# Reordering GpSimd's work in the turns of an attention stage: scatters without holds, the variance's power first

## The reference, cut to what matters

```
# stage 7, x is (8, 512, 256), 16 heads of 16
q = heads(layernorm(x) @ Wq.T + bq); k, v = heads(ctx @ Wk.T + bk), heads(ctx @ Wv.T + bv)
x = x + tanh(g_xattn[3]) * (softmax(q @ k.T / 4) @ v @ Wo.T + bo)
# stage 8
y = rmsnorm(layernorm(x)) * rms_w
vals, idx = top_k(y @ gate_w.T, 2); w = softmax(vals)
out = layernorm(x) + sum over the two experts e of w[e] * ((silu(y @ W1[e]) * (y @ W2[e])) @ W3[e])
x = x + tanh(g_ffn[3]) * out
```

## Time and profile before

| | |
|---|---|
| median of 3 runs | 2703.14 us (2701.21 to 2703.17) |
| the profiled execution, its own time | 2703.14 us |
| its span, first to last instruction | 2701.3 us |
| TensorE busy | 2433.2 us (90%) |
| VectorE busy | 1356.8 us (50%) |
| ScalarE busy | 943.6 us (35%) |
| GpSimd busy | 575.0 us (21%) |
| mean granted TensorE clock | 0.949 |
| stage 7 in the span | about 1837 to 2090 us |

### The profile page before, as it was taken

The page is one execution under the profiler, slowest core; times in us unless marked ns, Lnnn a source line. Parts: engine busy times, 40 slices in busy tenths (PEclk is TensorE's granted clock), DMA queues, the critical chain, the costliest instruction groups (busy, mean ns, idle before and its releaser), DMA issues.

```text
span 2701.3 us, 39252 instructions
## 1 busy us (share of the span) xinstructions
PE 2433.2 (90%) x13940; PEld 1598.6 (59%) x13940; DVE 1356.8 (50%) x3016; ACT 943.6 (35%) x2203; POOL 575.0 (21%) x544
## 2 busy tenths in 40 slices
PE   7997999999989987986999889986995899999998
PEld 4444766666666654444666654543553577777776
DVE  7886654754554556874222643336885323232322
ACT  2466555443444432321222212224553222222221
POOL 3234222440000102102321000002345212111111
PEclk9999999999999998997999669998996899999999
DMA  5013001220001102000000039302014322221221
GB/s 186 1 40 98 17 9 48 69 80 24 24 24 32 39 12 77 1 1 16 0 0 8 25 125 332 102 0 102 33 64 182 106 32 33 36 33 32 32 35 26
DMA packets 73747, 144.42 MB, mean 53 GB/s; under 512 B 11592, under 2 KB 62536, under 8 KB 71120
## 3 DMA queue, kind: packets, MB, share of 16 engines
q1 hardware_dynamic: 41280, 100.94, 10.9%
q0 software_dynamic: 16368, 26.23, 4.9%
q10 hardware_dynamic: 15936, 15.03, 2.0%
HBM read 107.42 MB, written 71.09 MB: 66 GB/s over the span
## 4 chain that ended last, share of the span: by engine, by line
PE 75%; DVE 10%; issue 6%; ACT 5%; DMA 1%; POOL 1%; another core or an unknown queue 0%; ACTq 0%; DVEq 0%; SPq 0%; POOLq 0%
PE PS L1959 12%; PE PS L1981 7%; PE PS L1382 4%; PE PS L1392 4%; PE PS L2347 4%; PE PS L1706 3%; PE PS L1717 3%; PE PS L564 3%; PE PS L2359 3%; PE PS L2381 3%; PE PS L2407 2%; PE PS L2442 2%; PE PS L2416 2%; PE PS L2452 2%; PE PS L639 2%
## 5 line engine op out<-in xcount | busy, mean ns | idle before, releaser
L1959 PE MATMUL PS<-mem,ctx2T 128*128 x1136 | 350.0, 461 | 2.1 <-ACT ctx2T L2022 1.1
L1959 PEld LDWEIGHTS PS<-mem,ctx2T 128*128 128x128 f32 x1136 | 211.4, 191 | 108.9 <-issue 4.3
L2141 POOL DMA_INDIRECT out_x<-xnT,moe_small x71 | 110.2, 1552 | 483.7 <-ACT xnT L2036 483.7
L1981 PE MATMUL PS<-mem,moe_small 128*128 x852 | 195.7, 379 | 1.1 <-DVE moe_small L2113 1.1
L2105 DVE TENSOR_TENSOR ctx2T<-PS,ctx2T 128x352 f32<-128x352 f32 x142 | 74.5, 524 | 243.1 <-PE PS L1959 243.1
L1981 PEld LDWEIGHTS PS<-mem,moe_small 128*128 128x128 f32 x852 | 156.4, 190 | 19.9 <-issue 1.4
L1056 DVE RECIPROCAL mem<-PS 128x512 f32<-128x512 f32 x48 | 160.8, 3350 | 12.6 <-PE PS L633 12.2
L2737 DVE TENSOR_REDUCE moe_small<-PS 128x2 f32<-128x1024 f32 x64 | 78.5, 1226 | 143.5 <-PE PS L2407 143.5
L2574 ACT ACTIVATE mem<-PS,moe_small 128x512 f32<-128x512 f32 x128 | 86.7, 682 | 158.2 <-DVE moe_small L2737 131.2
L1051 DVE TENSOR_REDUCE mem<-PS 128x32 f32<-128x2048 f32 x48 | 109.9, 2289 | 61.9 <-PE PS L589 61.7
L2110 DVE COPY moe_small<-PS 128x512 f32<-128x512 f32 x71 | 49.1, 691 | 173.2 <-PE PS L1969 173.2
(11 more groups left out here) (362 smaller groups left out, 4699.6 us busy)
## 6 DMA issues: line engine op xcount, KB each, us to landing
slots<-in_trash_rows SPq DMA_DIRECT2D x8, 4290.0 KB, 62.7
mem<-in_L_ffn_experts SPq DMA_DIRECT2D x8, 2176.0 KB, 8.9
xn<-unit_rows SPq DMA_DIRECT2D x15, 512.0 KB, 3.9
xn<-slots ACTq DMA_DIRECT2D x53, 130.0 KB, 2.1
x_all<-in_x SPq DMA_DIRECT2D x8, 512.0 KB, 8.3
mem<-unit_rows SPq DMA_DIRECT2D x8, 512.0 KB
out_x<-x_all ACTq DMA_DIRECT2D x8, 512.0 KB
unit_rows<-moe_small SPq DMA_DIRECT2D x7, 512.0 KB, 3.2
```

Of the source, the lines that this page charges most:

```text
L1959: last = nc.tensor.matmul(PS[:, 1 + 2 * g + half, 0:HE], m.rowT[:, j % 2, k, :], w[:, :, at:at + HE], start=k == 0, stop=k == KD - 1)
L1981: last = nc.tensor.matmul(PS[:, 7, 0:D], m.hT[:, j % 2, n, :], w[:, :, at:at + D], start=n == 0, stop=n == KE - 1)
L2141: nc.gpsimd.indirect_dma_start(s.T["out"], bass.IndirectOffsetOnAxis(s.token[:, j % 4:j % 4 + 1], 0), m.result[:, j % 4, :], None, compute ...
```

## The change

In the loop over the turns at the end of `xattn_pool`, `norm_powers` moves to the front of the turn and `scatter` up behind `row_ends`, ahead of `xn_scales` and `add_bias`. The two waits in the middle go: the one that let the first three scatters start only when TensorE had finished both of the turn's scores, and the one that let the other five start only when it had finished the shifted scores of the batch before. The eight scatters are one call.

```diff
     for n in range(s.turns):
         now, before, old, route, place = turn_of(s, n)
+        if route:
+            norm_powers(n - 3)
         if place:
             row_ends(n - 4)
+            scatter(n - 4, 0, 2 * TB)
         for b in STATS_IN_TURN.get(n, ()):
             xn_scales(b)
         if n + 1 < B:
             add_bias(n + 1)
-        if route:
-            norm_powers(n - 3)
-        if place:
-            if now:
-                pool.wait_ge(s.sems["scores"], 2 * n + 2)
-            scatter(n - 4, 0, 3)
-            if before:
-                pool.wait_ge(s.sems["shifted_psum"], 2 * n)
-            scatter(n - 4, 3, 2 * TB)
```

## The result

The changed kernel takes 2718.22 us (median of 4 runs, 2716.63 to 2719.6), the kernel before 2702.62 us (4 runs, 2701.21 to 2703.17): 1.0062 times, 95% interval 1.005 to 1.0075, some 16 us slower. The prediction was 2701.2 us with a range up to 2708.0: wrong. The profiled execution of the changed kernel took 2725.52 us, 7 us more than the median, so its sizes are too large: a later profile of the same kernel under the same conditions (2719.07 us) shows the stretches of turns 4 to 6 shorter by 0.7 to 3.2 us.

What follows compares the result with a forecast made beforehand. TensorE holds 75% of the last chain; results stall until the last scatter is dealt with. Turns 4 to 6: -4.5 + 4.5 = 0, turn 7 -1.4, turn 8 -0.5: -1.9 from 2703.14, 2701.2 us; range 2694.9 to 2708.

Steps and rivals of the forecast that it cites:

- Parts 1 and 2: GpSimd's turn: `norm_powers` first starts when it did, and nobody waits for `row_ends` behind it; worth 0 each.
- Part 3: Unheld scatters end 2.5 us earlier, so the stall goes: 1.5 us in each of turns 4 to 6, 1.4, then 0.5.
- Part 4: Turns 4 to 6: `add_bias` behind the scatters holds L1128 for 2.2 us, paying back 1.5 us a turn.
- Part 5: Turn 10: some 1.9 us of VectorE's wait for the power go without reaching the end; worth 0, at most 0.5.
- (c): Eight scatters in a row hold TensorE's results where all wait: +7.5, 2710.6 us; chance 0.16, with a clock loss.
- (b): Turns 4 to 8: the stall doesn't hang on the scatters' end and stays, hiding L1128's block: 2703.1 us; chance 0.14.
- (d): TensorE's clock after turn 5: shifted idle moves a half-speed stretch 1 to 2 us either way; loss shares (c)'s 0.16.
- (a): `add_bias` comes just after L1128, the stall still goes: -6.4, 2696.7 us; chance 0.22 all free, 0.12 partly.

Runs made afterwards that it cites:

- quiet comparisons: Three of six comparisons, those where the unaltered kernel before takes 2695 us; the changed kernel there takes 1.0035 and 1.0021 times that kernel's time.
- late comparisons: Three of six comparisons, the first measurement among them, where the unaltered kernel before takes 2702 to 2703 us; the changed kernel there takes 1.0062 times.
- The copies: Changed kernel plus SyncE copying 2.1 MB between DRAM tensors beside the scatters in turns 4 to 7: 2718.54 us, 1.0063 times the kernel before.
- bias_inside: Changed kernel with `add_bias` put between the second and third scatter, no holds: 1.0 times the kernel before (0.999 to 1.0009), 0.0 us.

## Why the prediction was wrong, step by step

**Parts 1 and 2 (power first, `row_ends` behind it: 0).** Right. The power starts when the variance is there, after an idle 18.18 us. The first scatter starts 11.95 us after the turn's first `add_out`, where the working had 1939.9 - 1928.37 = 11.5.

**Part 3 (holds removed: the stall goes, -6.4 us over turns 4 to 8).** This is the step that failed. Its arithmetic held: the scatters end 21.96 us after that `add_out` (predicted 21.5), and the pairs of L1066 are 1.64 us apart. But it took the 1.5 us that the kernel before showed for the whole effect, and asked only whether the results of the old place would be free in time. The effect is that TensorE's signals can arrive late while scatters run, in other places too. Once unheld, the scatters start ahead of the second scores' end, and the signals of these, of the sums and of the transposes come 2.7 to 5.3 us later than in the kernel before, one behind the other in the chain, and in part of the stretches the clock falls on top. The stretches of turns 4 to 6 became 8.3, 6.9 and 7.0 us longer in the profiled execution and 5.6, 3.7 and 6.3 in the later one, where 1.5 us were to go. In one comparison the removed holds alone cost 30.6 us (27 and 34 in its two runs), the order with the holds 0.5 us. In the quiet comparisons the step fails in another way: there is no stall to gain on. Two of the signs that the prediction named for being wrong came in the first profile: ScalarE waited longer, and L1128 took 0.19 us.

**Part 4 (`add_bias` behind the scatters blocks L1128 for 2.2 us).** The mechanism was right, and the first measurement didn't show it: there L1128 came at 1956.45 us instead of 1950.24, `add_bias` ran beside L1056 and L1059, and L1128 took 0.19 us. In the quiet comparisons it is the whole loss: L1124 loses 2.81 us, in turn 5 L1113 2.27 us. So the victim was named two instructions too late. The price, +1.5 us a turn, looked at `add_out` alone, where VectorE's wait of 0.77 us between the pairs takes up part of the block. That wait does go, but TensorE's rank matmuls (L673) wait for L1128 too: in four turns for 5.8 us, where the kernel before has one such wait of 2.5, and the stretch of turn 5 is granted a clock of 0.93. The turns pay 2.75, 2.33 and 1.91 us. With -1.9 us as the sum of the whole, the forecast would have missed the quiet +5.3 and +7.6 us as well.

The rule of the Trainium skill that the prediction cites here names a second input in SBUF as what makes the conflict; L1124, L1113 and L1149 agree. L1100 has one input, and lost 1.88 us. For this the same section of the Trainium skill ("SBUF — State Buffer", Who interferes with whom) says that `tensor_scalar` can enter a mode that uses both ports, and the row agrees.

**Part 5 (turn 10: 0).** Right. The power comes first, at 2094.92 us, and the first load of rows at 2122.47 us is 29.6 us behind the expert loads (before: 29.4). The timeline of turn 10:

```profile
2092.86 1.85 SPq L1906 DMA_DIRECT2D mem<-in_L_ffn_experts  x4
...
2094.92 1.68 POOL L1235 TENSOR_TENSOR moe_small<-moe_small 128x8 f32<-128x8 f32 x1 [8.00 <-DVE moe_small L1142]
```

**The rivals.** (c) came true in its kind and its sign; it had 0.16 together with a loss by the clock. Its place was wrong: it looked at the end of the row of scatters, "among the transposes of the maxima" (L601), and the late signals are those of L589, L633 and L652, 6 to 9 us ahead of it. It also kept the old stall, which went. Its price of 1.5 us a turn was the visible remainder of a late signal, where the holds had kept the rest away. The evidence against it, turn 10's eight scatters from 2076.32 us without a pause, is sound as far as it goes. The timeline of TensorE there, in the kernel before:

```profile
2081.62 3.58 PE L662 MATMUL PS<-moe_small,x_all 128*128 128x8 f32 x16 [0.78 <-ACT x_all L859]
```

The logits are over at 2085.20, and ScalarE reads them at 2085.24, with the scatters running; in the changed kernel turn 10 has no late signal either. So scatters alone don't make a signal late. Turn 10 differs in that TensorE stands still most of the time, and whether that is what matters wasn't tried. (b) fell in the late comparisons, since the stall went when the scatters moved. The rule of the Trainium skill quoted with it, that TensorE and ScalarE never wait for another's access, is neither borne out nor refuted: TensorE's matmuls kept their distances, and what came late is their results or the news of them. (d) was right as an addition and too small: TensorE's busy time in the stretch of turn 4 grew by 4.0 us (2.1 in the later profile). (a) was never met.

**What stays open.** What sets a comparison to late or quiet wasn't found. The copies were run in late conditions only, so whether more traffic could bring the lateness about in quiet ones is untested. Nor is the law of the lateness known. In the kernel before, in late conditions, the first three scatters run from 1941.50 to 1945.16 us, beside L622, L633 and L652, and none of these is late (L859 starts 0.72 us behind the start of L652), while in the changed kernel L589's signal, 0.8 us behind the first scatter's start, already is. `bias_inside` was not run in late conditions; with its holds gone nothing says that it would escape there, so it isn't offered as a better version. No kernel tried beats the kernel before in both.

## What to carry to other kernels

A wait that looks idle can be a fence: before it is taken out, list which signals of the bound engine will then fall beside the work that it held back, and don't price them by what is left of the wait with the fence in place: try the removal alone, in more than one comparison. When a GpSimd instruction of 2.4 us is moved, walk along VectorE's queue from 0.6 us ahead of its new start to its end and count every small instruction on SBUF as a possible victim, and then ask who else waits for that victim. Beside the long instructions that read PSUM it cost nothing here. A gain that rests on one stall in one profile should be checked for a second comparison in which that stall isn't there.

## What was unexpected in the hardware

- While GpSimd issues indirect DMAs (0.96 us each, 1.27 us from start to start), VectorE and ScalarE can get TensorE's results 2.7 to 5.3 us later than in the kernel before (turn 4, late conditions), or as promptly as ever (turn 10, and all quiet comparisons). The scatters themselves take equally long in both conditions.
- The same two kernels, with and without the holds, differ by 0.5 us or by 27 to 34 us, according to conditions that hold through a comparison and that the kernel before shows only as 2695 or 2702 us.
- The block can begin before GpSimd's record does: L1124 started 0.57 us ahead of `add_bias` and was still held to its end. Spans on GpSimd are rough, so it may be the record that begins late. The scatter before it didn't hold L1117, an instruction with two inputs in SBUF that ran inside it at its usual 0.23 us.
